# Attention heads multiplied in pairs on halves of the TensorE array, in place of zero-padded full-array matmuls

## The chip, the cores and the metric

The kernel runs on one core of a Trainium2 chip. The metric is the device time of one execution in microseconds (us). All arithmetic is fp32.

## What is computed

Eight sequences (B = 8) of T = 512 positions and D = 512 features pass two blocks. The first ("l0") is a linear attention with 16 heads of 32, a FiLM modulation and a residual. The second ("l1" and "mix") takes a modulated layer norm `xm` of that and computes a softmax attention beside a selective scan, and then one product of both. The part that the change touches is the softmax attention, 8 heads of 64:

```python
qkv = (xm @ Wqkv + bqkv).reshape(b, s, 3, H, hd)          # H = 8, hd = 64
q, k, v = (jnp.transpose(qkv[:, :, i], (0, 2, 1, 3)) for i in range(3))
att = jax.nn.softmax(jnp.einsum('bhqd,bhkd->bhqk', q * hd ** (-0.5), k), axis=-1)
out = jnp.einsum('bhqk,bhkd->bhqd', att, v)
```

## The kernel before, in words

The program has three stages, one after the other: `setup` (conditioning vectors, to about 75 us), `attend` (the softmax stage, to about 1670 us) and `mix` (the scan stage, the rest). Within a stage each engine has its own program, written out by hand, and semaphores join them; nothing is scheduled automatically.

`attend` first runs the first block for sequence 0 alone (`l0_alone`, to about 200 us). Then, for each sequence b, `l1(b, b + 1)` runs the softmax attention of sequence b with the first block of sequence b + 1 laid between its steps: `l0(n, g)` does what falls into slot g, and there are 33 slots. The last sequence has no partner.

In PE's `l1` the projections come first: `into_heads` (L780, products of 4 matmuls of 512 columns) makes q and k with the features on the partitions, two heads (a pair, `hp`, 0 to 3) to a block of 128; `into_values` makes v with the positions on the partitions. The first scores stand between them. Then each pair takes 8 half slots. In them PE does

- `scores(hp, t)` (L872), 16 times per sequence: for a block t of 128 queries, one matmul for each of the pair's two heads (e = 0, 1), each into its own PSUM bank (`sc_bank[e]`, two banks);
- `turns(hp, k, e)` (L878): four 128x128 transposes of the probabilities `PR`;
- `weighted(hp, k)` (L887), 16 times per sequence: for a block k of 128 keys, one matmul for each head of the pair, summed over k in one bank (`o_bank`).

A head has 64 features, and the array takes 128. Before, the head was padded with zeros: `Q2` has two planes, with head 0's queries above zeros in plane 0 and zeros above head 1's in plane 1, so that a contraction over all 128 partitions against the keys of both heads gives one head's scores. `V2` has 192 columns for each pair, head 0's values, 64 zeros, head 1's values; the 128 columns from 0 put head 0's result on partitions 0 to 63 and add zero to the others, and the 128 from 64 do the opposite, so both heads sum into the same bank:

```python
nc.tensor.matmul(sc_bank[e][:], Q2[:, e, hp, t * P:(t + 1) * P], K2[:, hp, :], start=True, stop=True)
nc.tensor.matmul(o_bank[:], V2[:, k, hp, e * DH1:e * DH1 + P], PT[:, k % 2, e, :], start=(k == 0 and e == 0), ...)
```

The other engines: VectorE scales q out of PSUM into `Q2` (`queries`, L697, one instruction for each half of the partitions), copies v into `V2` (`values`, L703), takes the row maxima of the scores (L709), inverts the sums (L713) and copies half of the turned probabilities to `PT` (L719). ScalarE makes the exponentials (L530) and copies the other half (L537). GpSimd multiplies the probabilities by the inverted sums (L447), and at the stage's start writes the zeros of `Q2` and `V2` (L429, L431), for which VectorE and PE wait (`pads_done`). PE waits before a score pair until both exponentials of the pair before are through (`pexp`). `r0` and `r1` are rings of PSUM banks (3 and 2), for the first block and for projections and transposes.

In the scan stage two matmuls are narrow already: `dt` (L1608) contracts over 64 rows, and the bias of the output projection (L1616) over one row. In the setup stage L248 has stationaries of 8 columns.

Of the kernel before, what the change touches and what calls it, by code (L numbers as in the profile page):

```python
# [24 lines left out]
P = 128  # L25
# [271 lines left out]
def attend(nc, a, bank, ident, cols, col, bq8, per_batch, x1_d, xm_d, ot_d, X, W, load, load_wide, arrived):  # L297
    ctx = ExitStack()
    with ctx:
        def sem(name):  # L300
            return ctx.enter_context(nc.semaphore(name))

        def sb(name, shape, dt=F32):
            return ctx.enter_context(nc.sbuf_tensor(name, shape, dt))
# [14 lines left out]
        cur = sb("cur", [P, NCUR])  # L319
        XM = sb("XM", [P, DC, T])  # L320
        V = XM
        Q2, K2 = sb("Q2", [P, 2, DC, T]), sb("K2", [P, DC, T])
        V2 = sb("V2", [P, TT, DC, 3 * DH1])
        OT = sb("OT", [P, DC, T])
        PR = sb("PR", [P, 2, 2, TT, T])
        PT = sb("PT", [P, 2, 2, T])
# [4 lines left out]

        bias_in = sem("bias_in")
        x_in, mask_in = arrived["x"], sem("mk_in")
        blocks_zero, blocks_done, pads_done = sem("blocks_zero"), sem("blocks_done"), sem("pads_done")
        cur_done, xb_done = sem("cur_done"), sem("xb_done")
        ln_var, ln_ln, ln_r0, ln_done = sem("ln_var"), sem("ln_ln"), sem("ln_r0"), sem("ln_done")
        xhat, yhat, x1hat = sem("xhat"), sem("yhat"), sem("x1hat")
# [41 lines left out]
        with nc.Block() as block:  # L379
# [39 lines left out]
            @block.gpsimd  # L419
            def _(pool):  # L420

                nc.gpsimd.memset(blocks[:], 0.0).then_inc(blocks_zero, 1)
                pool.wait_ge(blocks_zero, 1)
                for g in range(P // DH0):
                    s = slice(g * DH0, (g + 1) * DH0)
                    nc.gpsimd.memset(blocks[s, :, s], 1.0).then_inc(blocks_done, 1)
                pool.wait_ge(blocks_done, P // DH0)
                for e in range(2):
                    nc.gpsimd.memset(Q2[(1 - e) * DH1:(2 - e) * DH1, e], 0.0).then_inc(pads_done, 1)  # L429
                pool.wait_ge(pads_done, 2)  # L430
                nc.gpsimd.memset(V2[:, :, :, DH1:2 * DH1], 0.0).then_inc(pads_done, 1)  # L431
                pool.wait_ge(pads_done, 3)
                pool.wait_ge(bias_in, 3 * 16)

                def l0(n):
                    if n:
                        pool.wait_ge(*r0.done(n - 1, "x1", DC - 1))
                    nc.gpsimd.tensor_copy(cur[:], per_batch[:, n, :]).then_inc(cur_done, 1)
                    for t in range(TT):
                        pool.wait_ge(xhat, n * TT + t + 1)  # L440
                        nc.gpsimd.tensor_tensor(X[:, t, :], X[:, t, :], bias["film"][:], ALU.add).then_inc(xb_done, 1)

                def normalise(b, hp, t):
                    pool.wait_ge(rec_done, (b * PAIRS + hp) * TT + t + 1)
                    for e in range(2):
                        p = PR[:, hp % 2, e, t, :]
                        nc.gpsimd.tensor_tensor(p, p, rrec[:, hp % 2, t, e:e + 1].to_broadcast([P, T]), ALU.mult).then_inc(pnorm, 1)  # L447

                l0(0)
                for b in range(B):  # L450
                    for t in range(TT):
                        normalise(b, 0, t)
                    if b + 1 < B:
                        l0(b + 1)
                    for hp in range(1, PAIRS):
                        for t in range(TT):
                            normalise(b, hp, t)
# [123 lines left out]
            def _(dve):  # L581
# [110 lines left out]
                def l1(b, n):  # L692
                    def queries(i):
                        dve.wait_ge(r1.full, r1.at(b, "q", i))
                        for e in range(2):
                            s = slice(e * DH1, (e + 1) * DH1)
                            last = nc.vector.tensor_scalar(Q2[s, e, i, :], r1.bank(b, "q", i)[s, :], DH1 ** -0.5, bq8[s, i:i + 1], ALU.mult, ALU.add)  # L697
                        last.then_inc(r1.emptied["dve"], 1)

                    def values(t):  # L700
                        dve.wait_ge(r1.full, r1.at(b, "v", t))
                        v = V2[:, t].rearrange("p c (w d) -> p c w d", d=DH1)
                        nc.vector.tensor_copy(v[:, :, 0:3:2, :], r1.bank(b, "v", t)[:].rearrange("p (c w d) -> p c w d", w=2, d=DH1)).then_inc(  # L703
                            r1.emptied["dve"], 1)

                    def score_max(hp, t):
                        for e in range(2):
                            dve.wait_ge(sc_full, b * SC + (hp * TT + t) * 2 + e + 1)
                            nc.vector.tensor_reduce(nsmax[:, hp % 2, t, e:e + 1], sc_bank[e][:], AX, ALU.max, negate=True).then_inc(smax, 1)  # L709

                    def invert(hp, t):
                        dve.wait_ge(pexp, b * SC + (hp * TT + t + 1) * 2)
                        nc.vector.reciprocal(rrec[:, hp % 2, t, :], rsum[:, hp % 2, t, :]).then_inc(rec_done, 1)  # L713

                    def turned(hp, k):
                        if hp * TT + k >= 2:
                            dve.wait_ge(pv_done, (b * PAIRS + hp) * TT + k - 1)
                        dve.wait_ge(r1.full, r1.at(b, "t", hp, k, 0))
                        nc.vector.tensor_copy(PT[:, k % 2, 0, :], r1.bank(b, "t", hp, k, 0)[:]).then_inc(r1.emptied["dve"], 1)  # L719

                    queries(0)
                    queries(1)
                    if n is not None:
                        x_stats(n, 0)
                    score_max(0, 0)
                    if n is not None:
                        x_stats(n, 1)
                    score_max(0, 1)
                    queries(2)
                    invert(0, 0)  # L730
                    if n is not None:
                        x_stats(n, 2)
                    score_max(0, 2)
                    invert(0, 1)
                    if n is not None:
                        x_stats(n, 3)
                    score_max(0, 3)
                    queries(3)
                    invert(0, 2)
                    values(0)  # L740
                    if n is not None:
                        inv_std_end(n, 0)
                    invert(0, 3)
                    for t in range(1, TT):
                        values(t)
                    if n is not None:
                        l0(n, 0)
                    for hp in range(PAIRS):
                        for h in range(2 * TT):
                            if hp + 1 < PAIRS and h in SCORE:  # L750
                                score_max(hp + 1, SCORE[h])
                            if h % 2 == 0:
                                turned(hp, h // 2)
                            if hp + 1 < PAIRS and h in INVERT:
                                invert(hp + 1, INVERT[h])
                            if n is not None:
                                l0(n, 1 + hp * 2 * TT + h)

                dve.wait_ge(bias_in, 3 * 16)
                dve.wait_ge(blocks_done, P // DH0)  # L760
                dve.wait_ge(pads_done, 3)
                for t in range(TT):
                    x_stats(0, t)
                inv_std_end(0, 0)
# [6 lines left out]
            def _(pe):  # L771
# [84 lines left out]
                def l1(b, n):  # L856
# [9 lines left out]
                    def scores(hp, t):  # L866
                        if t == 0:
                            pe.wait_ge(*r1.done(b, "q", hp))
                            pe.wait_ge(*r1.done(b, "k", hp))
                        pe.wait_ge(pexp, b * SC + (hp * TT + t) * 2)  # L870
                        for e in range(2):
                            nc.tensor.matmul(sc_bank[e][:], Q2[:, e, hp, t * P:(t + 1) * P], K2[:, hp, :], start=True, stop=True).then_inc(sc_full, 1)  # L872

                    def turns(hp, k, e):
                        pe.wait_ge(pnorm, b * SC + (hp + 1) * 2 * TT - 1 + e)
# [5 lines left out]
                    def weighted(hp, k):  # L881
                        for e in range(2):
                            pe.wait_ge(*r1.done(b, "t", hp, k, e))
                        if k == 0:
                            pe.wait_ge(o_done, b * PAIRS + hp)
                        for e in range(2):
                            last = nc.tensor.matmul(o_bank[:], V2[:, k, hp, e * DH1:e * DH1 + P], PT[:, k % 2, e, :],  # L887
                                                    start=(k == 0 and e == 0), stop=(k == TT - 1 and e == 1))
                        last.then_inc(pv_done, 1)

                    pe.wait_ge(*r0.done(b, "x1", DC - 1))
# [27 lines left out]
                    weighted(PAIRS - 1, TT - 1)  # L919

                pe.wait_ge(blocks_done, P // DH0)
                pe.wait_ge(pads_done, 3)
                for name in ("L0_cond_Wk", "L0_cond_Wq", "L0_cond_Wv", "L0_cond_film_out_W"):
                    pe.wait_ge(arrived[name], 16)
                l0_alone(l0, 0)
# [794 lines left out]
```

## Time and profile before

| | |
|---|---|
| median of 3 runs | 4104.61 us (4102.66 to 4105.05) |
| the profiled execution | 4102.7 us |
| its span, first to last instruction | 4100.8 us |
| PE busy | 3529.0 us, 86% of the span |
| VectorE (DVE) busy | 2738.9 us, 67% |
| ScalarE (ACT) busy | 2036.7 us, 50% |
| GpSimd (POOL) busy | 1899.9 us, 46% |
| granted TensorE clock, mean | 0.907 |

PE is matmuls, PEld the weight loads, which run beside them. One matmul of the program on fp32 is two records in the trace (a transpose is one), so "x2" in an order of the program is "x4" in the trace. A record lasts longer than its share of PE, since records are pipelined: the time that one costs is read from start to start. "idle before" is the time in which an engine had nothing to do, with what ended it.

### The profile page before, as it was taken

What the parts mean: (1) busy time and instruction counts of PE and PEld (TensorE: products, weight loads), DVE (VectorE), ACT (ScalarE), POOL (GpSimd) and SP (SyncE); (2) the same over time, 40 slices, a digit from 0 to 9 for tenths busy, and PEclk for the clock granted to TensorE, in tenths of its full rate; (3) what the DMA queues carried; (4) which work ended last, traced back from release to release, by engine and by line L of the source; (5) the groups of instructions that cost most, each with busy time, mean ns of one, the idle gap of its engine ahead of it and who ended that gap; (6) DMA issues with size and microseconds to landing.
All of it is one profiled execution on the core that took longest, in us unless ns stands there. A gap on an engine that the chain in (4) does not pass through costs nothing.

```text
span 4100.8 us, 36398 instructions
## 1 busy us (share of the span) xinstructions
PE 3529.0 (86%) x12362; PEld 1915.2 (47%) x12362; DVE 2738.9 (67%) x3491; ACT 2036.7 (50%) x3486; POOL 1899.9 (46%) x1142
## 2 busy tenths in 40 slices
PE   5799999999999999767888888888888888888858
PEld 1445455454545454344454454444444544444543
DVE  1343434343434343279899799899898897997992
ACT  1233333333333333474676667656655755766542
POOL 1021212121221212195676677667667756767760
PEclk8899999999999999867889889898899898898859
DMA  5001010101010101111213222222222132121111
GB/s 197 34 1 44 1 44 0 44 1 44 1 44 1 44 11 62 38 42 61 73 63 98 67 73 82 73 84 80 65 90 80 63 113 70 62 96 59 42 59 41
DMA packets 100937, 230.04 MB, mean 56 GB/s; under 512 B 10305, under 2 KB 10417, under 8 KB 97682
## 3 DMA queue, kind: packets, MB, share of 16 engines
q1 hardware_dynamic: 97186, 220.50, 16.1%
q10 hardware_dynamic: 3568, 7.21, 0.5%
q8 instruction: 101, 1.65, 0.2%
q14 instruction: 82, 0.67, 0.1%
HBM read 193.85 MB, written 33.83 MB: 56 GB/s over the span
## 4 chain that ended last, share of the span: by engine, by line
PE 18%; POOL 14%; DVE 12%; issue 12%; ACT 3%; DMA 0%; POOLq 0%; SPq 0%; DVEq 0%; ACTq 0%
POOL HS L1181 10%; PE bank L1542 10%; DVE HS L1420 6%; DVE acc L1425 5%; PE bank L1618 3%; PE bank L1559 3%; PE bank L1616 1%; POOL delta L1196 1%; POOL ZS L1187 1%; DVE U L1457 1%; POOL DU L1199 1%; ACT bank L1258 1%; POOL comb L1212 1%; PE bank L1568 0%; POOL comb L1215 0%
## 5 line engine op out<-in xcount | busy, mean ns | idle before, releaser
L1181 POOL TENSOR_TENSOR HS<-DU,brep 128x1024 f32<-128x1024 f32 x512 | 1197.5, 2357 | 635.8 <-PE bank L1559 635.8
L1420 DVE TENSOR_TENSOR_SCAN HS<-bank,HS 128x1024 f32<-128x1024 f32 x512 | 1167.8, 2281 | 71.2 <-ACT bank L1258 58.5
L1559 PE MATMUL bank<-ident,HS 128*128 128x128 f32 x4096 | 686.9, 319 | 342.0 <-DVE acc L1425 307.0
L1258 ACT ACTIVATE bank<-delta,aneg 128x511 f32<-128x511 f32 x1024 | 662.1, 680 | 501.6 <-DVE HS L1420 499.5
L1559 PEld LDWEIGHTS bank<-ident,HS 128*128 128x128 f32 x4096 | 559.0, 164 | 617.7 <-DVE HS L1420 401.4
L447 POOL TENSOR_TENSOR PR<-PR,rrec 128x512 f32<-128x512 f32 x256 | 260.4, 1041 | 1264.5 <-DVE rrec L713 1264.5
L1425 DVE SCALAR_TENSOR_TENSOR acc<-bank,C,acc 128x512 f32<-128x512 f32 x960 | 667.1, 737 | 135.4 <-PE bank L1559 133.9
L1542 PE MATMUL bank<-XM,w_l 128*128 128x512 f32 x1024 | 498.9, 635 | 43.1 <-DVE U L1457 19.1
L1542 PE MATMUL bank<-w_l,G 128*128 128x512 f32 x1024 | 476.6, 611 | 7.3 <-ACT delta L1268 3.9
L530 ACT ACTIVATE PR<-bank,nsmax 128x512 f32<-128x512 f32 x256 | 174.7, 685 | 425.1 <-DVE nsmax L709 419.8
L780 PE MATMUL bank<-w_l,NT 128*128 128x512 f32 x768 | 355.0, 607 | 5.6 <-ACT NT L478 5.5
L1542 PEld LDWEIGHTS bank<-XM,w_l 128*128 128x128 f32 x1024 | 200.7, 206 | 267.3 <-issue 218.4
L1542 PEld LDWEIGHTS bank<-w_l,G 128*128 128x128 f32 x1024 | 194.2, 199 | 212.8 <-issue 204.4
L872 PE MATMUL bank<-K,Q 128*128 128x512 f32 x512 | 244.1, 599 | 21.1 <-ACT PR L530 17.9
L887 PE MATMUL bank<-PT,V 128*128 128x512 f32 x512 | 239.7, 593 | 0.0
L780 PE MATMUL bank<-XM,w_l 128*128 128x512 f32 x512 | 228.2, 596 | 1.0 <-ACT XM L478 1.0
L780 PEld LDWEIGHTS bank<-w_l,NT 128*128 128x128 f32 x768 | 144.9, 195 | 167.8 <-issue 159.8
L709 DVE TENSOR_REDUCE nsmax<-bank 128x1 f32<-128x512 f32 x256 | 170.4, 687 | 71.8 <-PE bank L872 71.4
L878 PEld LDWEIGHTS bank<-ident,PR 128*128 128x128 f32 x1024 | 126.2, 142 | 98.3 <-issue 91.5
L1457 DVE SCALAR_TENSOR_TENSOR U<-bank,convw,U 128x509 f32<-128x509 f32 (+2 forms) x192 | 143.1, 746 | 28.6 <-ACT U L1317 23.5
L719 DVE COPY PT<-bank 128x512 f32<-128x512 f32 x128 | 87.7, 685 | 108.5 <-PE bank L878 108.2
L780 PEld LDWEIGHTS bank<-XM,w_l 128*128 128x128 f32 x512 | 98.0, 192 | 124.4 <-issue 124.4
(171 smaller groups left out, 4007.5 us busy)
## 6 DMA issues: line engine op xcount, KB each, us to landing
brep<-b_d SPq DMA_DIRECT2D x256, 256.0 KB, 3.2
w_l<-in_L_cond_W_in SPq DMA_DIRECT2D x14, 2048.0 KB, 9.7
w_l<-in_L_cond_W_full SPq DMA_DIRECT2D x8, 2048.0 KB, 8.6
w_l<-in_L_cond_W_out SPq DMA_DIRECT2D x7, 2048.0 KB, 9.7
X<-in_x SPq DMA_DIRECT2D x8, 1024.0 KB, 5.2
x_d<-X SPq DMA_DIRECT2D x8, 1024.0 KB, 4.8
xm_d<-XM SPq DMA_DIRECT2D x8, 1024.0 KB, 4.3
ot_d<-OT SPq DMA_DIRECT2D x8, 1024.0 KB, 3.8
```

Source lines behind the costliest of these rows:

```text
L447: nc.gpsimd.tensor_tensor(p, p, rrec[:, hp % 2, t, e:e + 1].to_broadcast([P, T]), ALU.mult).then_inc(pnorm, 1)
L530: nc.scalar.activation(PR[:, hp % 2, e, t, :], sc_bank[e][:], ACT.Exp, bias=nsmax[:, hp % 2, t, e:e + 1], accum_out=rsum[:, hp % 2, t, e:e ...
L780: last = nc.tensor.matmul(dst[:], lhs(c), rhs(c), start=(c == 0), stop=(c == DC - 1))
L872: nc.tensor.matmul(sc_bank[e][:], Q2[:, e, hp, t * P:(t + 1) * P], K2[:, hp, :], start=True, stop=True).then_inc(sc_full, 1)
L887: last = nc.tensor.matmul(o_bank[:], V2[:, k, hp, e * DH1:e * DH1 + P], PT[:, k % 2, e, :], start=(k == 0 and e == 0), stop=(k == TT - 1 a ...
L1181: nc.gpsimd.tensor_tensor(HS[:, u % DEEP], DU[:, chunks(j, s), :], brep[:, m % 3, :].unsqueeze(1).to_broadcast([P, UC, T]), ALU.mult).then ...
L1258: last = nc.scalar.activation(dA[:, s, i, 1:T], delta[:, c, 1:T], ACT.Exp, scale=aneg[:, c, n:n + 1])
L1420: nc.vector.tensor_tensor_scan(h, dA[:, u % 2].rearrange("p i t -> p (i t)"), h, 0.0, ALU.mult, ALU.add).then_inc(scanned, 1)
L1425: nc.vector.scalar_tensor_tensor(out=acc[:, t, :], in0=y_bank[t % 2][:], scalar=C[:, j // 2 % 2, t, n:n + 1], in1=acc[:, t, :], op0=ALU.mu ...
L1457: last = nc.vector.scalar_tensor_tensor(out=y, in0=ring.bank(n, f"xr{c}")[:, 0:T - lag], scalar=convw[:, c, k:k + 1], in1=y, op0=ALU.mult, ...
L1542: last = nc.tensor.matmul(dst, lhs(c), rhs(c), start=(c == 0), stop=(c == of - 1))
L1559: last = nc.tensor.transpose(y_bank[t % 2][:, i * P:(i + 1) * P], h, ident[:])
```

## The change

`Q2` loses its planes and `V2` its zero columns. A score matmul contracts over the 64 partitions of its own head, for queries and keys alike. A weighted matmul has a stationary of 64 columns and writes the 64 partitions of `o_bank` that belong to its head; the two heads are two sums of their own. The built program gives the scores an array tile of 64 rows by 128 columns, at row 0 or 64, and the weighted matmuls one of 128 rows by 64 columns, at column 0 or 64. VectorE scales q in one instruction, and the zeros with their semaphore are gone.

```diff
-        Q2, K2 = sb("Q2", [P, 2, DC, T]), sb("K2", [P, DC, T])
-        V2 = sb("V2", [P, TT, DC, 3 * DH1])
+        Q2, K2 = sb("Q2", [P, DC, T]), sb("K2", [P, DC, T])
+        V2 = sb("V2", [P, TT, D])
...
-                for e in range(2):
-                    nc.gpsimd.memset(Q2[(1 - e) * DH1:(2 - e) * DH1, e], 0.0).then_inc(pads_done, 1)
-                pool.wait_ge(pads_done, 2)
-                nc.gpsimd.memset(V2[:, :, :, DH1:2 * DH1], 0.0).then_inc(pads_done, 1)
-                pool.wait_ge(pads_done, 3)
...
-                        for e in range(2):
-                            s = slice(e * DH1, (e + 1) * DH1)
-                            last = nc.vector.tensor_scalar(Q2[s, e, i, :], r1.bank(b, "q", i)[s, :], DH1 ** -0.5, bq8[s, i:i + 1], ALU.mult, ALU.add)
-                        last.then_inc(r1.emptied["dve"], 1)
+                        nc.vector.tensor_scalar(Q2[:, i, :], r1.bank(b, "q", i)[:], DH1 ** -0.5, bq8[:, i:i + 1], ALU.mult, ALU.add).then_inc(
+                            r1.emptied["dve"], 1)
...
-                        v = V2[:, t].rearrange("p c (w d) -> p c w d", d=DH1)
-                        nc.vector.tensor_copy(v[:, :, 0:3:2, :], r1.bank(b, "v", t)[:].rearrange("p (c w d) -> p c w d", w=2, d=DH1)).then_inc(
-                            r1.emptied["dve"], 1)
+                        nc.vector.tensor_copy(V2[:, t, :], r1.bank(b, "v", t)[:]).then_inc(r1.emptied["dve"], 1)
...
                         for e in range(2):
-                            nc.tensor.matmul(sc_bank[e][:], Q2[:, e, hp, t * P:(t + 1) * P], K2[:, hp, :], start=True, stop=True).then_inc(sc_full, 1)
+                            s = slice(e * DH1, (e + 1) * DH1)
+                            nc.tensor.matmul(sc_bank[e][:], Q2[s, hp, t * P:(t + 1) * P], K2[s, hp, :], start=True, stop=True).then_inc(sc_full, 1)
...
                         for e in range(2):
-                            last = nc.tensor.matmul(o_bank[:], V2[:, k, hp, e * DH1:e * DH1 + P], PT[:, k % 2, e, :],
-                                                    start=(k == 0 and e == 0), stop=(k == TT - 1 and e == 1))
+                            f = slice((2 * hp + e) * DH1, (2 * hp + e + 1) * DH1)
+                            last = nc.tensor.matmul(o_bank[e * DH1:(e + 1) * DH1, :], V2[:, k, f], PT[:, k % 2, e, :],
+                                                    start=(k == 0), stop=(k == TT - 1))
```

The three waits for `pads_done` on VectorE, PE and GpSimd go too.

The order of the instructions stays. On PE in the changed program, a piece of sequence 0's attention (L863 are scores, L869 transposes of probabilities, L879 weighted matmuls, L765 and L770 transposes and products; a row's size is that of the output):

```order
L765 MATMUL bank<-ident,H 128x128 x4
L863 MATMUL bank<-K,Q 128x512 x2
L869 MATMUL bank<-ident,PR 128x128 x4
L879 MATMUL bank<-PT,V 64x512 x2
L770 MATMUL bank<-NT,w_l 128x512 x4
L869 MATMUL bank<-ident,PR 128x128 x4
L770 MATMUL bank<-NT,w_l 128x512 x4
L863 MATMUL bank<-K,Q 128x512 x2
L869 MATMUL bank<-ident,PR 128x128 x4
L879 MATMUL bank<-PT,V 64x512 x2
```

Only the size of the weighted matmul's output differs from before (128x512 there). Each pair on halves stands between work on the full array. At the end of each sequence two weighted pairs follow each other:

```order
L765 MATMUL bank<-ident,H 128x128 x8
L869 MATMUL bank<-ident,PR 128x128 x4
L765 MATMUL bank<-ident,H 128x128 x8
L869 MATMUL bank<-ident,PR 128x128 x4
L879 MATMUL bank<-PT,V 64x512 x4
```

These four matmuls are the only longer run on halves.

## Rows read from the trace of the kernel before

**Rows 1.** Two of the page's rows of 40 slices, busy tenths and clock.

```profile
PE   5799999999999999767888888888888888888858
...
PEclk8899999999999999867889889898899898898859
```

**Rows 2.** Windows: one batch of the softmax stage, columns in the header.

```profile
core 0: us, PE busy (x) PEld busy (x) DVE busy (x) ACT busy (x) POOL busy (x), PEclk, DMA share, GB/s
...
740.00:933.00 193.00, 185.30 (x621) 96.75 (x620) 79.96 (x164) 67.53 (x139) 37.16 (x37) 0.98 0.07 24
```

**Rows 3.** The waits of PE in 740 to 933 us: us, times, longest.

```profile
PE bank L775 <- ACT H L474: 2.7, 2, 2.2
PE bank L775 <- ACT NT L478: 2.4, 1, 2.4
PE bank L872 <- ACT PR L530: 2.0, 2, 1.2
```

**Rows 4.** Groups by line to 1700 us: busy us, mean ns, idle before.

```profile
L872 PE MATMUL bank<-K,Q 128*128 128x512 f32 x512 | 244.1, 599 | 21.1 <-ACT PR L530 17.9 <-DVE V L703 3.2
L887 PE MATMUL bank<-PT,V 128*128 128x512 f32 x512 | 239.7, 593 | 0.0
...
L887 PEld LDWEIGHTS bank<-PT,V 128*128 128x128 f32 x512 | 87.8, 190 | 65.3 <-issue 65.0
```

**Rows 5.** Timeline of PE, last batch: start us, us, what.

```profile
1630.45 1.88 PE L887 MATMUL bank<-PT,V 128*128 128x512 f32 x4
1632.17 1.88 PE L872 MATMUL bank<-K,Q 128*128 128x512 f32 x4
```

**Rows 6.** Timeline of PE in the scan stage, around L1608.

```profile
2237.46 1.04 PE L1559 MATMUL bank<-ident,HS 128*128 128x128 f32 x8
2238.33 3.60 PE L1542 MATMUL bank<-XM,w_l 128*128 128x512 f32 x8
2241.76 1.04 PE L1559 MATMUL bank<-ident,HS 128*128 128x128 f32 x8
2242.73 1.12 PE L1608 MATMUL bank<-xdbl,small 64*128 64x512 f32 x2
2243.78 1.09 PE L1559 MATMUL bank<-ident,HS 128*128 128x128 f32 x8
2244.81 1.12 PE L1608 MATMUL bank<-xdbl,small 64*128 64x512 f32 x2
```

**Rows 7.** Timeline of PE in the scan stage, around L1616.

```profile
2017.34 1.04 PE L1559 MATMUL bank<-ident,HS 128*128 128x128 f32 x8
2018.31 1.12 PE L1616 MATMUL bank<-small 1*128 1x512 f32 x2
2019.36 3.70 PE L1618 MATMUL bank<-w_l,comb 128*128 128x512 f32 x8
2022.90 0.27 PE L1559 MATMUL bank<-ident,HS 128*128 128x128 f32 x1
```

**Rows 8.** Timeline of the setup stage, stationaries of 8 columns.

```profile
65.58 3.60 PE L248 MATMUL bank<-wada,condT 128*8 128x512 f32 x8
```

**Rows 9.** Line L697, durations ns; then who waited for line L703.

```profile
L697 DVE TENSOR_SCALAR Q<-bank,bq x64: 742/750/759, 199.0 to 1578.3; 64x512 f32<-64x512 f32 x64
...
  PE bank L872: 3.2, 8
```

**Rows 10.** Timeline at the softmax stage's start, and a DMA's landing.

```profile
75.90 0.45 ACTq L463 DMA_DIRECT2D bias_film<-in_L_cond_film_out_b  x1
...
80.33 0.96 POOL L431 MEMSET V<- 128x1024 f32 x1
...
81.49 2.47 DVE L585 BATCH_NORM_STATS2 stats<-X 128x6 f32<-128x512 f32 x4 [6.96 <-POOL V L431]
...
bias_film<-in_L_cond_film_out_b ACTq DMA_DIRECT2D x1, 256.0 KB, 4.9
```

**Rows 11.** Window in the scan stage around L1608; columns as in rows 2.

```profile
2241.00:2252.00 11.00, 8.19 (x45) 4.84 (x43) 10.89 (x10) 9.77 (x17) 8.58 (x4) 1.00 0.15 35
```

More of the change, by code:

```diff
@@ L333, in attend @@
         x_in, mask_in = arrived["x"], sem("mk_in")
-        blocks_zero, blocks_done, pads_done = sem("blocks_zero"), sem("blocks_done"), sem("pads_done")
+        blocks_zero, blocks_done = sem("blocks_zero"), sem("blocks_done")
         cur_done, xb_done = sem("cur_done"), sem("xb_done")
@@ L760, in _ @@
                 dve.wait_ge(blocks_done, P // DH0)
-                dve.wait_ge(pads_done, 3)
                 for t in range(TT):
@@ L921, in _ @@
                 pe.wait_ge(blocks_done, P // DH0)
-                pe.wait_ge(pads_done, 3)
                 for name in ("L0_cond_Wk", "L0_cond_Wq", "L0_cond_Wv", "L0_cond_film_out_W"):
```

## The prediction

> **What bounds the kernel now.** I read the page first, then the windows, then single stretches of the timeline. In the page's slices of the softmax stage (about 200 to 1670 us) TensorE (PE) is busy nine tenths or more almost throughout, with a granted clock of nine tenths or more [rows 1]. In the windows one batch of this stage lasts 193.0 us, of which PE works 185.3, VectorE 80.0, ScalarE 67.5 and GpSimd 37.2 [rows 2]. So PE is the bound here, and what is taken from or added to PE's stream is taken from or added to the time. The waits say how nearly: of the 7.7 us that PE is idle in a batch, 2.7 and 2.4 us go to ScalarE's H and NT and only 2.0 us stand before the score matmuls [rows 3]. The scan stage behind it is bound by other things and is not touched; it starts when the softmax stage ends, and shifts as a whole.
>
> The work in question: L872 (scores) and L887 (weighted sum) have 512 matmul records each [rows 4]. A program matmul on fp32 is two records, so there are 256 of each, 32 of each per batch, in pairs (head 0, head 1). In the timeline a pair is "x4", and from its start to the next start is 1.72 us: 0.43 us a record [rows 5]. All pairs together: 256 pairs x 1.72 = 440 us on the bounding engine.
>
> **Part 1: what leaving the padding gives.** A score matmul now uses 64 rows of the array, the other head's the other 64; a weighted matmul uses 64 columns, the other head's the other 64. The number of matmuls and their moving length (512) stay. A single narrow matmul gains nothing by itself: 8 records with a stationary of 8 columns take 3.60 us [rows 8], just as 8 full ones do [rows 6], and 64-row and 1-row records stream no faster either (below). All the gain is in overlap of the halves. Order on PE is a1, a2 (head 0's two records), b1, b2 (head 1's). If records start in that order and one half can't begin its second record before its first is through, a2 and b1 run together and nothing else does: three steps in place of four. That saves 0.43 us a pair. At a batch's end two weighted pairs stand side by side (L887 x4 in the order), where eight steps become five, one more saved. Saved steps: 256 + 8 = 264, x 0.43 = 113 us. No row of before shows two matmuls on different halves, so the overlap is unproven; bounds are 0 and, with both records overlapped, 512 steps, 220 us. I take 113, since every row of PE shows starts in program order.
>
> **Part 2: what going to half an array and back costs.** The trace does show this: the scan stage has single matmuls of 64 rows (L1608) and of one row (L1616) between full-array work. Undisturbed, 8 transposes take 0.87 us from start to start and 8 full records 3.43 [rows 6]. The cycle "two 64-row records, 8 transposes" takes from 2242.73 to 2244.81, 2.08 us, where 0.86 + 0.87 = 1.73 would do: 0.35 us for leaving and returning. It is spread as 0.10 ahead (2241.76 to 2242.73), 0.19 on the half (2242.73 to 2243.78 is 1.05) and the rest on the transposes behind. The one-row case has a 512-wide product behind it, which itself is prolonged (2019.36 to 2022.90, 3.54 in place of 3.43), and pays 0.10 + 0.19 + 0.11 = 0.40 [rows 7]. So about 0.2 us each way: PE runs empty, then the first weight load lies open. It doesn't come per matmul, since the second record shows no further loss.
>
> The changed kernel makes such a trip for each pair, because transposes or products on the full array stand around every one. Trips: 16 for scores and 15 for weighted in a batch, 31 x 8 = 248. Scores: 12 of 16 have transposes behind (0.35), 4 a product (0.40): 0.36 x 128 = 46 us. Weighted trips have a first load of half the columns; no row prices a column trip, so its bounds are 0 (rows 8 stays on one kind of tile and proves nothing of switching) and 0.40; I take 0.33, nearest to the row trips: x 120 = 40 us. Cost 86 us, of which the waits that already stand before scores (21.1 us in all, [rows 4]) can hide a little; I count nothing for it.
>
> **Part 3: the rest.** VectorE's two half-width scalings of Q (64 x 0.75 us, nobody waited for them) become one, and the copy of V loses its stride [rows 9]; both lie beside PE, 0. They bring the first scores no earlier either: their wait is for the last V copy, 3.2 us over 8 batches [rows 9], which stays. The last memset of the pads ends at 80.33 + 0.96 = 81.29, and VectorE's first statistics start at 81.49; but VectorE also waits for the third bias, issued at 75.90 and 4.9 us on its way, 80.80 [rows 10]. Gain 0.5 us. With less to do per pair on PE, the next thing late would be ScalarE's exponentials, which guard the two score banks; they have slack (67.5 of 193), so 0. PE's clock stays at its upper level, 2.4 GHz (PEclk 1.00), in a window of the scan stage with 64-row records, transposes and 2.8 us of idle in 11 [rows 11]; the softmax stage is denser, and I expect no change of level.
>
> Sum: -113 + 86 - 0.5 = -28 us. Against the profiled execution's 4102.7 us that is 4074.7; the median of the runs, 4104.6, stands 1.9 higher, so 4076 or, with the little hidden in waits, **4075 us**.
>
> **The rivals.**
> *The halves don't overlap at all (ends slower).* Place: every pair. Price: the 86 us of trips with nothing against it, 4104.6 + 85 = 4190, some 4186 with what waits hide. The deciding point is sharp: a trip costs 0.35 and the overlap gives 0.43, so if fewer than about 80% of pairs overlap, the change loses. For it: nothing in the trace shows an overlap, and fp32 in two records may hold the array. Against: the halves share neither rows nor banks in the scores. Chance 0.21.
> *Only one kind overlaps.* If scores do and weighted pairs (both moving streams enter the same 128 rows, both results go to one bank) don't: -55 + 86 = +31, 4135; the other way round -58 + 86 = +28, 4132. Chance 0.13.
> *The weight loads of a column pair lie open.* Each load of a half array waits until the matmul before it is through, and costs the 0.1 us priced above: three more loads in each of 128 weighted pairs, +38, 4075 + 38 = 4113. For it only that a first load after a trip lies open; against, on the full array a record's load of 0.19 us [rows 4] stands beside matmuls at 0.43 with nothing added, and the second 64-row record shows no loss. Chance 0.05. The Trainium skill (TensorE: Matmul & The Clock Gate, "Part 3: Packing small matmuls — row/col tiling") has such a rule: a weight load overlaps running matmuls only where it goes to other rows, which a column pair's loads don't. For the full array the trace disagrees with it.
> *Both records overlap, four steps become two.* -220 + 86 = -134, 3970. It needs b1 to start beside a1, past a2. For it, only that the halves are independent; against, starts in order in every row. Chance 0.08. The Trainium skill (TensorEngine Tiling, "Theoretical Speedup") gives this factor, up to 2; the first page says that matmuls start and end strictly in order, by which it would be my three steps.
> *The change doesn't do what it says:* the records run as on a full array with idle rows, neither trip nor overlap. 4104. The 64-row rows [rows 6] speak against it. Chance 0.03.
>
> **How the numbers follow.** My forecast has 0.50: its own range is 4040 (column trips nearly free, -35) to 4090. Faster holds it and the two-step case, 0.58. Same (within 0.2%, about 8 us, which is what a measurement of this kernel can tell) holds the case that nothing changes and a little of the open loads, 0.05. Slower is the rest of 0.21 + 0.13 + 0.05, 0.37. To keep 8 in 10 the range must take in the serial case, so it runs from 4040 to 4190 and leaves the two-step case out.
>
> **What would show it.** In the profile after: from the start of a score pair to the next start about 1.29 + 0.19 (before: 1.72), 0.10 more ahead of it and some 0.06 behind; the starts of b1 and a2 within a few hundredths. A batch of 190 us in place of 193. DVE L697's successor x32. If a pair takes 1.9 us or more from start to start, the serial case holds; if it takes about 1.05, the two-step case. If batches shorten by much less than PE's own work, a wait on ScalarE has taken its place. The stage behind should be unchanged in length.

## The result and the profile after

The changed kernel takes 4014.01 us (median, 4012.57 to 4018.89) against 4104.83 us before, timed again beside it: a ratio of 0.978 (95% interval 0.976 to 0.980), 90.8 us faster. I had forecast 28 us, in a range that ended at 4040; the time came out below it. The profiled execution has a span of 4013.2 us, 87.6 less than before. All times here are medians of fast runs; one slow run of e1 (4701.9 us, at a granted clock of 0.71) is left out of its median.

The timeline of PE in the last sequence of the changed kernel (start us, us, what), to be held against [rows 5] and, for single narrow matmuls, [rows 6]:

```profile
1544.78 0.66 PE L869 MATMUL bank<-ident,PR 128*128 128x128 f32 x4
1545.52 1.13 PE L863 MATMUL bank<-K,Q 64*128 64x512 f32 x4
1546.58 0.66 PE L869 MATMUL bank<-ident,PR 128*128 128x128 f32 x4
1547.16 1.08 PE L879 MATMUL bank<-PT,V 128*64 128x512 f32 x4
1548.17 0.33 PE L869 MATMUL bank<-ident,PR 128*128 128x128 f32 x1
```

Four score records (L863) take 1.06 us from start to start, where they took 1.72, and four weighted records (L879) 1.01. One record lasts 0.43, so 1.06 has room for two steps (0.86) and 0.20 of opening and closing, and not for three. The records of line L863 counted in short windows show the two steps (us, PE busy with the records that run, PEld busy, clock, DMA):

```profile
1545.50:1545.60 0.10, 0.08 (x2) 0.09 (x2) 1.00 0.00 0
1545.60:1546.00 0.40, 0.40 (x2) 0.21 (x4) 1.00 0.00 0
1546.00:1546.10 0.10, 0.10 (x4) 0.00 (x0) 1.00 0.00 0
```

Two records start together, no other starts for 0.4 us, then the other two start together. The four weight loads of the pair fit this on the load queue:

```profile
1545.51 0.30 PEld L863 LDWEIGHTS bank<-K,Q 64*128 64x128 f32 x4 [0.31 <-ACT PR L525]
```

All four are done in 0.30 us, less than the 0.43 of one step: head 1's loads don't wait until head 0's matmuls are through. The groups of the stage, which answer to [rows 4]:

```profile
L869 PE MATMUL bank<-ident,PR 128*128 128x128 f32 x1024 | 163.6, 287 | 3.7 <-ACT PT L532 2.0 <-DVE PT L710 1.3 <-POOL PR L442 0.3
L863 PE MATMUL bank<-K,Q 64*128 64x512 f32 x512 | 146.3, 648 | 37.3 <-ACT PR L525 33.7 <-DVE V L695 3.2
L879 PE MATMUL bank<-PT,V 128*64 128x512 f32 x512 | 141.0, 631 | 1.0 <-ACT PT L532 1.0
```

Both kinds of pair fell by about 98 us of busy time, from 244.1 and 239.7. Idle time before the scores rose from 21.1 to 37.3 us. The waits of PE in the whole stage, first before (200 to 1668 us), then after (200 to 1582 us), each us in total, times, longest:

```profile
PE bank L775 <- ACT H L474: 18.7, 14, 2.2
PE bank L872 <- ACT PR L530: 17.9, 18, 1.2
PE bank L775 <- ACT NT L478: 16.6, 7, 2.4
PE bank L780 <- ACT NT L478: 4.6, 5, 0.9
PE bank L872 <- DVE V L703: 3.2, 8, 0.8
PE bank L800 <- DVE KT L647: 2.5, 7, 0.4
```

```profile
PE bank L863 <- ACT PR L525: 33.7, 25, 2.3
PE bank L765 <- ACT H L469: 29.1, 14, 3.3
PE bank L765 <- ACT NT L473: 14.0, 7, 2.4
PE bank L790 <- DVE KT L642: 11.0, 7, 1.6
PE bank L770 <- ACT NT L473: 3.7, 4, 0.9
PE bank L863 <- DVE V L695: 3.2, 8, 0.8
```

These rows sum to 63.5 and 94.7 us; with the small ones left out (0.3 and 4.6) 63.8 and 99.3, so 35.5 us more waiting: PE's own work shrank, the chains on the other engines did not. The stretches of the stage by windows (columns as in [rows 2]), before and after:

```profile
205.00:1668.00 1463.00, 1395.09 (x4699) 723.31 (x4697) 606.49 (x1236) 523.02 (x1074) 295.61 (x291) 0.99 0.07 25
```

```profile
205.00:1582.00 1377.00, 1271.66 (x4692) 606.41 (x4692) 572.38 (x1204) 517.10 (x1074) 295.18 (x291) 0.97 0.07 26
```

VectorE does 34 us less. The last weighted matmuls of the stage end at 1663.99 us before and at 1576.65 after, 87.3 earlier, and from there to the end of the span are 2436.8 and 2436.5 us: the scan stage is as long as before. A batch lasts about 183 us in place of 193; the prediction had 190.

The mean granted clock of the stage has fallen from 0.99 to 0.97 of the upper level, 2.4 GHz. In short windows it is nearly always 1.00 or 0.50, the lower level of 1.2 GHz. The profile has the lower level for 24 us of the stage before (200 to 1664 us), in 7 stretches, and for 72 us after, in 16. One of them stands behind a wait of PE before a score pair; timeline, then windows:

```profile
1064.35 1.13 PE L863 MATMUL bank<-K,Q 64*128 64x512 f32 x4 [2.31 <-ACT PR L525]
1065.41 0.68 PE L869 MATMUL bank<-ident,PR 128*128 128x128 f32 x4
1066.02 1.98 PE L879 MATMUL bank<-PT,V 128*64 128x512 f32 x4
```

```profile
1055.00:1066.00 11.00, 8.69 (x52) 4.64 (x50) 8.29 (x24) 4.81 (x14) 4.07 (x4) 1.00 0.00 1
1066.00:1076.00 10.00, 7.96 (x27) 4.93 (x27) 2.53 (x6) 9.95 (x15) 2.30 (x3) 0.50 0.01 2
```

The weighted pair lasts 1.98 us there in place of 1.08. If half of PE's busy time at the lower level counts as lost, the stage lost 11 us before and 33 after. That is my estimate of the clock's price in the change: 21 us.

### The profile page after: what moved, and what is told of

The parts are those of the page before. It is cut to its first block, busy times and chain, and to the rows that moved or that the text cites. A ratio compares the mean times of both kernels' runs of the same rounds, so it can differ in the third digit from the quotient of the medians.

```text
span 4013.2 us, 36362 instructions
## 1 busy us (share of the span) xinstructions
PE 3408.5 (85%) x12362; PEld 1798.9 (45%) x12362; DVE 2704.5 (67%) x3459; ACT 2030.8 (51%) x3486; POOL 1894.0 (47%) x1139
## 4 chain that ended last, share of the span: by engine, by line
PE 18%; POOL 14%; DVE 13%; issue 13%; ACT 3%; DMA 0%; POOLq 0%; SPq 0%; DVEq 0%; ACTq 0%
POOL HS L1172 11%; PE bank L1533 10%; DVE HS L1411 6%; DVE acc L1416 5%; PE bank L1609 4%; PE bank L1550 3%; PE bank L1607 1%; POOL delta L1187 1%; POOL ZS L1178 1%; DVE U L1448 1%; POOL DU L1190 1%; ACT bank L1249 1%; POOL comb L1203 1%; PE bank L1559 0%; POOL comb L1206 0%
## 5 line engine op out<-in xcount | busy, mean ns | idle before, releaser
L770 PE MATMUL bank<-w_l,NT 128*128 128x512 f32 x768 | 360.6, 615 | 4.7 <-ACT NT L473 4.5
L770 PE MATMUL bank<-XM,w_l 128*128 128x512 f32 x512 | 232.5, 605 | 1.0 <-ACT XM L473 1.0
L770 PEld LDWEIGHTS bank<-w_l,NT 128*128 128x128 f32 x768 | 143.6, 196 | 178.0 <-issue 159.3
L869 PEld LDWEIGHTS bank<-ident,PR 128*128 128x128 f32 x1024 | 120.5, 146 | 133.9 <-issue 100.8
L863 PE MATMUL bank<-K,Q 64*128 64x512 f32 x512 | 146.3, 648 | 37.3 <-ACT PR L525 33.7
L869 PE MATMUL bank<-ident,PR 128*128 128x128 f32 x1024 | 163.6, 287 | 3.7 <-ACT PT L532 2.0
L770 PEld LDWEIGHTS bank<-XM,w_l 128*128 128x128 f32 x512 | 94.8, 191 | 135.9 <-issue 135.9
```

Of the source, the lines that this page charges most:

```text
L770: last = nc.tensor.matmul(dst[:], lhs(c), rhs(c), start=(c == 0), stop=(c == DC - 1))
L869: last = nc.tensor.transpose(r1.bank(b, "t", hp, k, e)[:, t * P:(t + 1) * P], PR[:, hp % 2, e, t, k * P:(k + 1) * P], ident[:])
```

## The experiments

Each is timed against the kernel before on the same chip; e1 to e4, e5 to e8, e9 and e10, and e11 ran on four different chips, on which the kernel before takes 4103.3 to 4105.1 us.

**e1, e2: one kind alone.** e1 keeps the halves for the scores and the padded `V2`, e2 the halves for the weighted sum and the padded `Q2`.

```diff
 e1, against the kernel before
-        Q2, K2 = sb("Q2", [P, 2, DC, T]), sb("K2", [P, DC, T])
+        Q2, K2 = sb("Q2", [P, DC, T]), sb("K2", [P, DC, T])
         V2 = sb("V2", [P, TT, DC, 3 * DH1])
...
 e2, against the kernel before
         Q2, K2 = sb("Q2", [P, 2, DC, T]), sb("K2", [P, DC, T])
-        V2 = sb("V2", [P, TT, DC, 3 * DH1])
+        V2 = sb("V2", [P, TT, D])
...
```

> Theory A (a pair on halves runs wholly together, two steps in place of four; each trip to halves and back costs about 0.35 us, and PE's waits before the scores grow): the scores save 256 steps x 0.43 = 110 us, pay 128 x 0.36 = 46 us and lose some 30 us to waits, 30 to 40 us under before, 4065 to 4075 us. Theory B (only one step of four overlaps in a pair, and the remaining gain of the change comes from elsewhere): 55 - 46 = 9 us or less under before, 4095 or more. Score pairs from start to next start: A 1.06 us, B 1.48.

> Theory A: 256 steps x 0.43 = 110 us saved, 120 trips x 0.33 = 40 us paid, few waits since the weighted pairs wait for nothing: 55 to 70 us under before, 4035 to 4050 us. With e1 it adds up to the change's 91 us, give or take 10. Theory B: 58 - 40 = 18 us or less under before, 4087 or more.

Measured: e1 4061.9 us (ratio 0.989, 0.988 to 0.991), 43 us under before; e2 4057.0 (0.989, 0.987 to 0.990), 48 us under. Together 91, as much as the change: both kinds overlap, and the two add up. In e1 the score pairs take 1.06 us from start to start and the weighted ones 1.72, in e2 1.72 and 1.01. e1 gained a little more than theory A's 30 to 40, since its waits grew by 22 us and not by 30. e2 gained less than theory A said, which had left the waits out for it: with e2 they grow by 24 us.

**e3: the rest undone.**

```diff
+                for e in range(2):
+                    nc.gpsimd.memset(Q2[(1 - e) * DH1:(2 - e) * DH1], 0.0).then_inc(pads_done, 1)
...
+                nc.gpsimd.memset(V2[:, :, 0:D // 2], 0.0).then_inc(pads_done, 1)
...
+                            last = nc.vector.tensor_scalar(Q2[s, i, :], r1.bank(b, "q", i)[s, :], DH1 ** -0.5, bq8[s, i:i + 1], ALU.mult, ALU.add)
```

> The change with the memsets and their waits put back (on tiles that are overwritten later) and Q scaled in two instructions of 64 partitions. Theory A: all of the gain is PE's, so this is within 3 us of the change, 4014 to 4017 us. Theory B: the missing gain was VectorE's freed 24 us and the earlier start, so this is 20 us or more slower than the change.

Measured: 4015.3 us (0.978, 0.977 to 0.980), 1.3 over the change. The copy of V keeps its new form here, but it takes 0.69 us before and after alike. So VectorE's and GpSimd's savings are worth nothing that counts; all is PE's.

**e4: the overlap taken away, the halves kept.**

```diff
-                                scores(hp + 1, SCORE[h])
+                                scores(hp + 1, SCORE[h], (0,))
                             turns(hp, k, e)
+                            if hp + 1 < PAIRS and h in SCORE:
+                                scores(hp + 1, SCORE[h], (1,))
```

> In the 12 of 16 score pairs that lie in the pair loop, the four transposes stand between head 0's and head 1's matmul. Theory A: 96 pairs lose two steps of 0.43 us (82 us) and make a second trip (34 us): up to 116 us over the change, 4110 to 4130 us, a little less where PE waited anyhow. If narrow matmuls were faster by themselves and the overlap only apparent: only the trips, 34 us over the change, 4048 us.

Measured: 4109.3 us (1.001, 1.000 to 1.002), 95 us over the change, just under theory A's 4110. The timeline of e4 (start us, us, what):

```profile
904.61 1.12 PE L863 MATMUL bank<-K,Q 64*128 64x512 f32 x2
905.66 0.66 PE L869 MATMUL bank<-ident,PR 128*128 128x128 f32 x4
906.25 1.12 PE L863 MATMUL bank<-K,Q 64*128 64x512 f32 x2
907.30 1.08 PE L879 MATMUL bank<-PT,V 128*64 128x512 f32 x4
```

One head alone takes 1.05 us from start to start, as much as both together took (1.06). So the two records that start together in the changed kernel are one of each head, since one head's two records alone need two steps. Splitting 96 of 128 score pairs gives back about as much as the whole change: a half array by itself is no faster. Not all of the 95 us are steps and trips: the clock's lower level lasts 123 us in e4's stage, in place of 72, which by the same estimate costs 27 us, and PE is idle for 34 us less.

**e5, e6: trips alone.** The kernel before, with one matmul of each pair on half the array and the other padded. In e6 the padded one comes first, and the half one adds to it.

```diff
 e5, scores
+                            s = slice(0, P) if e else slice(0, DH1)
+                            nc.tensor.matmul(sc_bank[e][:], Q2[s, e, hp, t * P:(t + 1) * P], K2[s, hp, :], start=True, stop=True).then_inc(sc_full, 1)
 e6, weighted sum, head 0
+                                last = nc.tensor.matmul(o_bank[0:DH1, :], V2[:, k, hp, 0:DH1], PT[:, k % 2, e, :],
+                                                        start=False, stop=(k == TT - 1), skip_group_check=True)
```

> The kernel before, with head 0's score matmul alone on 64 rows (queries and keys of partitions 0 to 63), head 1's padded as before: a trip for each pair and nothing to overlap. Theory A (a trip costs 0.35 to 0.40 us): 128 trips, 46 us over before, 4151 us; a little less where PE waited anyhow. This is what the prediction's serial case priced. Theory C (trips cost less than the scan stage's rows say, and that is the missing gain): under 20 us over before, 4125 or less.

> The kernel before, with head 1's padded weighted matmul first and head 0's behind it on 64 columns, adding to partitions 0 to 63. Theory A (a column trip costs as much as a row trip, less 0.05 for the shorter load): 120 to 128 trips x 0.33, 40 us over before, 4145 us. Theory C (column trips are free): 4105 us, within 5.

Measured: e5 4142.9 us (1.010, 1.008 to 1.011), 38 over before, 0.30 a trip; e6 4128.3 (1.006, 1.004 to 1.007), 23 over, 0.18 a trip. Column trips are not free, but both kinds cost less in the time of the whole kernel than on PE's timeline. The timeline of e5 has for one pair:

```profile
1648.09 0.60 PE L879 MATMUL bank<-ident,PR 128*128 128x128 f32 x4
1648.62 2.18 PE L873 MATMUL bank<-K,Q 64*128 64x512 f32 x4
1650.63 0.60 PE L879 MATMUL bank<-ident,PR 128*128 128x128 f32 x4
```

From 1648.09 to 1650.63 are 2.54 us, where 0.44 + 1.72 would do: 0.38 for the trip. The timeline of e6 has:

```profile
1624.81 1.02 PE L888 MATMUL bank<-PT,V 128*128 128x512 f32 x2
1625.76 1.07 PE L891 MATMUL bank<-PT,V 128*64 128x512 f32 x2
1626.77 0.66 PE L878 MATMUL bank<-ident,PR 128*128 128x128 f32 x4
1627.26 1.88 PE L872 MATMUL bank<-K,Q 128*128 128x512 f32 x4
```

From 1624.81 to 1627.26 are 2.45 us, where 1.72 + 0.44 would do: 0.29 for the trip, 0.06 less than the row trip of [rows 6]; part 2 had taken 0.33. In e6 that is 37 us for 128 trips, where the profiled execution shows the stage ending 24 us later. The rest is in the profile: PE's waits in the stage fell by 5 us, so part of the price is paid in time that PE waited before, and the clock's lower level lasted 10 us in place of 24, worth 6 us by the same estimate.

**e7, e8: how far PE looks ahead.** Weighted pairs of two key blocks side by side, issued in half slots 1 and 5 of a pair; in e8 head 0's two first.

```diff
-        PT = sb("PT", [P, 2, 2, T])
+        PT = sb("PT", [P, TT, 2, T])
...
+                        for j, e in [(j, e) for j in (k, k + 1) for e in range(2)]:
...
 e8
+                        for j, e in [(j, e) for e in range(2) for j in (k, k + 1)]:
```

> The change, with the weighted pairs of two key blocks side by side (four buffers for the turned probabilities in place of two): 64 trips in place of 120. Theory A: 56 trips x 0.33 saved, 18 us under the change, 3996 us. If trips are cheap (theory C): within 5 us of the change. If the later weighted pairs hold something up: slower than the change.

> As e7, but in each group of four weighted matmuls head 0's two come first, then head 1's two (a, a', b, b'). If matmuls of the program start in order and only neighbours can overlap: a alone, a' with b, b' alone, six steps in place of four, 64 x 0.86 = 55 us over e7, 4051 us. If PE looks past a waiting matmul of the same half for one of the other half: as e7, 3996 us.

Measured: e7 3999.6 us (0.975, 0.973 to 0.976), 14 under the change, where theory A said 18: PE's waits grew from 99 to 104 us, which is the difference; e8 4001.3 (0.975, 0.973 to 0.977), the same as e7. The timeline of e8:

```profile
1557.60 1.94 PE L879 MATMUL bank<-PT,V 128*64 128x512 f32 x8
1559.47 1.09 PE L869 MATMUL bank<-ident,PR 128*128 128x128 f32 x8
```

Eight records in the order a1 a2 a'1 a'2 b1 b2 b'1 b'2 take 1.87 us: four steps of 0.43 and 0.15. Head 0's four records need four steps on their half, so head 1's four must stand beside them one by one: its first record is fifth in the program and ran beside the first of head 0. The timeline cut off at 1557.99 has two records already:

```profile
1557.60 0.66 PE L879 MATMUL bank<-PT,V 128*64 128x512 f32 x2
```

Each half works off its own row of matmuls; what waits for head 0's half doesn't hold up head 1's.

**e9, e10: the waits before the scores.** On top of e7; e9 issues odd scores behind the transposes of their half slot, e10 spreads the scores.

```diff
 e9, PE
-                            if hp + 1 < PAIRS and h in SCORE:
+                            if hp + 1 < PAIRS and h in SCORE and e == 0:
                                 scores(hp + 1, SCORE[h])
                             turns(hp, k, e)
...
+                            if hp + 1 < PAIRS and h in SCORE and e == 1:
+                                scores(hp + 1, SCORE[h])
 e10
-        SCORE, INVERT = {0: 0, 1: 1, 3: 2, 5: 3}, {1: 0, 2: 1, 4: 2, 6: 3}
+        SCORE, INVERT = {0: 0, 2: 1, 4: 2, 6: 3}, {1: 0, 3: 1, 5: 2, 7: 3}
```

> e7 with the scores of odd half slots issued behind that half slot's transposes, so that 5 of 16 score pairs per sequence stand directly before a weighted group and pass from rows to columns without full-array work between. If a change of tile shape costs the same 0.15 to 0.2 us whichever two shapes it joins, each saves one of four changes: 40 x 0.15 = 6 us, and the scores' wait for the exponentials (38.0 us in e7) shrinks by up to 0.6 us a piece: 3980 to 3994 us. Rival: passing from rows to columns needs no change at all, then 12 us from that. If the waits are only moved: as e7, 3999.6 us.

> e7 with the next pair's scores at half slots 0, 2, 4, 6 in place of 0, 1, 3, 5, and the inversions at 1, 3, 5, 7. Theory A says that the two-step case lost some 35 us to waits, half of it before scores that follow each other too closely for ScalarE's exponentials (38.0 us in e7). Spread, these waits should halve: 15 to 20 us under e7, 3980 to 3985 us. Rival: the last scores then come too late for GpSimd's normalising, and the wait moves to the first transposes of the next pair: within 5 us of e7 or slower.

Measured: e9 4006.8 us (0.976, 0.974 to 0.978), e10 4013.6 (0.978, 0.977 to 0.979): e10 is slower than e7, e9 no faster (its interval overlaps e7's), and both forecasts of theory A failed. The waits moved. The longest of e9, then of e10 (200 to 1567 us):

```profile
PE bank L869 <- ACT PT L532: 41.3, 21, 3.1
...
PE bank L863 <- ACT PR L525: 7.3, 10, 1.2
```

```profile
PE bank L765 <- ACT H L469: 40.9, 14, 3.9
PE bank L863 <- ACT PR L525: 24.8, 20, 2.1
PE bank L790 <- DVE KT L642: 13.5, 7, 1.9
```

In e9 the wait before the scores all but vanished (38.0 us in e7) and stood again before the transposes, since ScalarE made the late exponentials ahead of the copy of turned probabilities, for which the ring of banks waits. In e10 the first block of the next sequence pays; the rival had foretold a slower kernel, but with the wait on GpSimd's normalising, which is 3.6 us.

**e11: ScalarE in PE's order.**

```diff
-                            if hp + 1 < PAIRS and h in SCORE:
+                            if hp + 1 < PAIRS and h in SCORE and e == 0:
                                 probabilities(hp + 1, SCORE[h])
                             if e == 1:
                                 turned(hp, k)
+                            if hp + 1 < PAIRS and h in SCORE and e == 1:
+                                probabilities(hp + 1, SCORE[h])
```

> e9 with ScalarE in PE's new order: in odd half slots it copies the turned probabilities first and makes the exponentials behind. In e9 PE waited 41.3 us for that copy (transposes on ScalarE's PT), against 38.0 us before the scores in e7. If the lost time of e9 was this order: most of the 41.3 us goes, 3965 to 3985 us. If PE then waits before the scores again (the wait moves a second time): 3995 to 4005 us.

Measured: 3982.8 us (0.970, 0.969 to 0.972), 24 us under e9 and 31 under the change. It is the fastest kernel of this study. Its longest waits:

```profile
PE bank L865 <- ACT PR L525: 29.4, 27, 2.1
PE bank L767 <- ACT H L469: 18.0, 8, 2.4
```

So the order on ScalarE was what e9 had lost by; some of the wait before the scores is back. In the stage PE is idle for 14 us less than in e9, and the clock's lower level lasts 48 us in place of 72. Score pairs now stand directly before a weighted group:

```profile
966.90 1.13 PE L865 MATMUL bank<-K,Q 64*128 64x512 f32 x4
967.96 1.94 PE L881 MATMUL bank<-PT,V 128*64 128x512 f32 x8
969.83 3.70 PE L772 MATMUL bank<-NT,w_l 128*128 128x512 f32 x8
```

The scores take 1.06 us to the next start, and the group 1.87, as they do between transposes: the passage from rows to columns costs the opening of the columns and no more. What it saves in time was not isolated from the order.

## Why the prediction was wrong

The step that failed is in part 1: "If records start in that order ..., a2 and b1 run together and nothing else does: three steps in place of four." I took it because "every row of PE shows starts in program order". In those rows no two matmuls stand on different halves, so they say nothing of this case. The runs showed two steps (1.06 us a score pair, 1.01 a weighted one), with the records starting two by two, and e8 shows that the program's order between the halves doesn't matter at all. The case stood among the rivals, with a chance of 0.08 and a time of 3970; the range left it out on purpose. The Trainium skill (TensorE: Matmul & The Clock Gate, "Part 3: Packing small matmuls — row/col tiling") says that matmuls never reorder; I let it support the three steps. Between halves e8's 1.87 us for eight records is against it. The Trainium skill (TensorEngine Tiling (Array Packing), "Theoretical Speedup") gives a factor of up to 2, and PE's steps show it here, two for four.

The errors partly hid each other. 248 steps more than the forecast's 264 would have put the time 107 us under it; waits and clock gave about half of that back, and the time came out 61 us under.

The rival's own time, 3970, was 44 us too low. With 512 steps saved (-220 us) and trips at 86:

- The trips' price held on PE's timeline. The cycle of a score pair and four transposes is 1546.58 + 0.58 - 1545.52 = 1.64, where 0.86 + 0.44 = 1.30 would do: 0.34 for the 0.35 of part 2. The column trip, which no row priced, is 0.29 for 0.33 (e6). With these two prices, 128 row trips and 120 column trips are 78 us and not 86. That trips on one matmul of each pair cost the kernel before only 38 and 23 us (e5, e6) puts its serial case at about 4166, an estimate, and not 4186.
- "With less to do per pair on PE, the next thing late would be ScalarE's exponentials ... they have slack (67.5 of 193), so 0": the first half was right, the 0 wrong. Waits grew by 35.5 us, 15.8 of them before the scores. This is the second step that failed. Slack in a window's sum (67.5 of 193) says nothing of a chain with two banks that runs scores, maximum, exponential and back. e9 to e11 show the same from the other side.
- "I expect no change of level" of the clock: the lower level lasted 72 us of the stage in place of 24, and costs 21 us more by the estimate above. -220 + 78 + 35.5 + 21 = -85.5, against the 87.3 by which the stage ended earlier in the profile. The sum closes within 2 us. The clock's share is worked out from the profile; no run changed the clock alone. The prediction went by one window of 11 us at the upper level [rows 11], too little to speak for a whole stage with more waits in it.
- The rest: 0.5 us forecast, 1.3 measured (e3), a difference that the intervals can't tell. In the changed kernel VectorE's first statistics wait for the bias, as foretold.

Right were what bounds the stage, that a narrow matmul alone gains nothing (e4), that trips come per change of tile and not per matmul, and that the scan stage only shifts.

## What to carry to other kernels

Two matmuls that each fill half of the array, on rows or on columns, run together when they stand next to each other with nothing of the full array between them, and together take the time of one. That is shown for fp32 with 512 moving columns, on two tiles of 64 rows and on two of 64 columns. Count the changes of tile shape, 0.15 to 0.2 us each way, and gather narrow pairs into groups (e7), since each trip costs a third or more of the 0.86 us that the overlap gives. Where the bounding engine is relieved by a tenth, price the waits too: follow one chain through its banks instead of comparing busy sums. And look at the granted clock in short windows, since new waits can come with time at the lower level, as 48 us more of it did here.

## What the runs showed of the hardware

The halves take their matmuls independently, though an fp32 matmul is two records, and past three records that wait for the other half (e8). A pair of weighted records on columns is a little cheaper to open than a score pair on rows (1.01 against 1.06), in step with its weight load of 64 columns for 128. The two weighted pairs' second set showed no further cost: eight records in 1.87 us are 0.15 over four steps, just what four records pay.
